# Four stages of a two-layer perceiver kernel rearranged: values folded into the output projection, a joined projection stage, a narrower reciprocal, another order of waits

## The chip, the core and the metric

The kernel runs on one core of one Trainium2 chip. The metric is the device time of one launch in microseconds. Before the change it is 2432.17 us, the median of three runs (2431.6 to 2434.42). TensorE is the matmul engine (PE in the profile, its weight loads PEld), VectorE is DVE, ScalarE is ACT, GpSimd is POOL, SyncE is SP.

## What is computed

128 batches of 32 tokens of width 128, all in float32, held as 32 tiles of 128 rows (4 batches each). Two layers follow one another; their parts are a gated unit over context rows, a linear attention, a block with attention over the batch and eight experts, a cross attention over 257 context rows, a clamped attention with normed queries and keys, and routed experts. The parts that the change touches:

```python
# linear attention, 16 heads of 64, x normed
q = softmax(q, axis=-2) * SCALE ; k = softmax(k, axis=-1)      # q over features, k over tokens
context = einsum('bhdn,bhen->bhde', k, v)
out = einsum('bhde,bhdn->bhen', context, q) @ w_out + b_out

# end of the batch attention block
proj = ao @ proj_weight.T ; h1 = hidden_states + proj
ln2 = layer_norm(h1, ln2_weight, ln2_bias) ; logits = ln2 @ router_weight

# cross attention: softmax of scores over 257 keys, times v, then w_out
# clamped attention: q, k of unit length, 50 * tanh(s / 50), causal softmax, times v, w_out
```

## The kernel before

All stages are written out as one instruction stream for each engine, with semaphores between engines; an engine executes its stream strictly in the written order. A stage is a block; between two blocks all engines meet. `steps(eng, n, body)` runs the first three tiles unrolled, then a hardware loop of two tiles a turn, then the last tile. `wait(eng, sem, value)` is a semaphore wait.

**stage_linear_attention** (137.7 to 541.5 us). Tile t, half h (8 heads each). TensorE per half: q (L495), transposes of the softmaxed q of the half before (L513), k (L500), o of the tile before (L546), v (L506), x transpose of the next tile in the first half (L489), y of the tile before in the second half (L553), A of the half before (L528). A is the 32 x 32 product of softmaxed k and q for each batch and head; o is v times A, 64 small products a half; y multiplies o, transposed, by w_out: eight 128x128 products accumulated. ScalarE: A copies (L602), q_T copy (L609), exp of q (L622), four o copies of 128 columns (L594), exp of k (L626), v copy (L629), x_T copy (L588). VectorE: sums, maxima, differences and reciprocals of both softmaxes (L698 to L712, L676, L681), the norm of the next tile (L666) and the residual add with statistics (L109, L111). GpSimd: bias add (L649), k norm (L645), q softmax (L656).

**stage_projection** (from 807.2 us) runs tile by tile: ScalarE stages the attention output (L1436), TensorE multiplies (L1444), VectorE adds to the hidden rows and takes statistics (L1451, L1453), GpSimd adds them to X (L1462); at the end 32 aggregations (L104). Then `deviation_phase` (square root L129, reciprocal L138), then `stage_norm_transpose`: norm (L1150), transpose (L1130), copy with weight and bias (L1142), router product (L1125) for each tile, and one eviction of all logits (L1154).

**stage_cross_attention** (to about 1750 us) runs in units of one batch, j = 0 to 3 in a tile. TensorE in a unit: scores of four head groups, each in its own 32-row strip (L2055), transposes of p of the unit before (L2113), k of the next unit (L2064), a transpose of the reciprocals (L2073) and p times v of two units before (L2077), v (L2086), and at the end x transpose (L2093), q (L2098) or y (L2105). VectorE in a unit: masked scores with their minimum for four groups (L2335), k rotations (L2324, L2325), two p_T copies (L2342), o mixed (L2355), o kept, called xat_o (L2364), and last the reciprocal of the row sums, written 32 times wide (L2348), so that its transpose lines up with o; then in one unit each the norm, the q products or the residual add. ScalarE: p_T copies (L2224), four exponentials (L2211), v copy (L2203), the last p column spread 32 wide, called p_last (L2218).

**stage_clamped_attention** (1752 to 2131.5 us). Per half, TensorE: q (L820), kv (L825), transposes of the scaled q and k of the half before (L836), then in the first half o transposes (L873) and the x transpose of the next tile (L810), in the second half y (L881); then scores of the half before (L850) and p times v of two halves before (L865). VectorE: o_norm (L1050, L1053), scale (L1033, L1036), sums of squares (L1079, L1082), in the first half the norm of the next tile (L1025), the lower bound of the sums (L1088), the q_T copy (L1044), in the second half the residual add. GpSimd: the power -1/2 of the bounded sums (L1011), the mask on p (L995), a sum of heads (L988). The x transpose waits for the norm of its tile.

Of the kernel before, what the change touches and what calls it, by code (L numbers as in the profile page):

```python
# [17 lines left out]
ALU = mybir.AluOpType  # L18
# [6 lines left out]
P = 128  # L25
# [396 lines left out]
def stage_linear_attention(nc, k, w, wo, bo, ahead):  # L422
# [5 lines left out]
    with ExitStack() as ctx:  # L428
# [15 lines left out]
        vs = [sb(f"v{i}", [P, W]) for i in range(2)]  # L444
        am = [sb(f"A_T{i}", [P, HALF, S]) for i in range(2)]
        oT = [sb(f"o_T{i}", [P, 2, NC, P]) for i in range(2)]
# [6 lines left out]
        pQ, pK, pV, pQT = k.bank[0:4]  # L453
        pB = k.bank[4:8]
        OC, MC = slice(0, P), slice(P, 2 * P)
        pA, pX, pY = pB[0:2], pB[2], pB[3]
# [5 lines left out]
        q_made, k_made, v_made = sem("q_made"), sem("k_made"), sem("v_made")  # L462
# [4 lines left out]
        v_copied = sem("v_copied")  # L467
# [3 lines left out]
        o_made, o_copied = sem("o_made"), sem("o_copied")  # L471
# [3 lines left out]
        block = ctx.enter_context(nc.Block())  # L475

# [8 lines left out]
        def _(pe):  # L485
            def x_transpose(t, slot):
                pe.wait_ge(normed, t + 1)
                wait(pe, o_copied, BT * (2 * (t - 1) - 1))
                pe.transpose(pX[:, MC], xn[slot][:, :], k.ident[:, :]).then_inc(turned, 1)  # L489
# [14 lines left out]
            def v(t, slot, h):  # L504
                wait(pe, v_copied, unit(t, h))
                pe.matmul(pV[:, :], xT[slot][:, :], w[:, 2, h, :], start=True, stop=True).then_inc(v_made, 1)  # L506
# [9 lines left out]
            def a(t, h):  # L516
# [4 lines left out]
                wait(pe, o_copied, BT * u)  # L521
                pe.sem_inc(pe_waited, 1)
                for i in range(NC):
                    for half in range(2):
                        r = slice(DH * half, DH * half + DH)
                        for b in range(BT):
                            n = slice(S * b, S * b + S)
                            m = pe.matmul(pA[half][n, P + i * S:P + (i + 1) * S], ks[h][r, i, n], qT[h][r, i, n],  # L528
# [4 lines left out]
            def o(t, h):  # L533
                u = unit(t, h)
                pe.wait_ge(v_copied, u + 1)
                pe.wait_ge(a_copied, 2 * u + 2)
                if h == 0:
                    wait(pe, added, 2 * (t - 1) + 1)
                wait(pe, o_copied, BT * u)
                pe.sem_inc(pe_waited, 1)  # L540
                for c in range(NC):
                    for b in range(BT):
                        n = slice(S * b, S * b + S)
                        for half in range(2):
                            hd = 2 * c + half
                            m = pe.matmul(pB[b][DH * half:DH * half + DH, c * S:(c + 1) * S],  # L546
                                          vs[h][n, hd * DH:(hd + 1) * DH], am[h][n, hd, :], start=True, stop=True)
                m.then_inc(o_made, 1)

            def y(t, slot):  # L550
                pe.wait_ge(o_copied, BT * (2 * t + 2))
                for c in range(2 * NC):
                    m = pe.matmul(pY[:, MC], oT[slot][:, c // NC, c % NC, :], wo[:, c, :],  # L553
                                  start=(c == 0), stop=(c == 2 * NC - 1))
                m.then_inc(y_made, 1)

            def body(t, slot, first, last):
                if first:
                    x_transpose(t, slot)
                for h in range(2):  # L560
# [5 lines left out]
                    if not first:  # L566
                        o(t - 1, h)
                    v(t, slot, h)
                    if h == 0 and not last:
                        x_transpose(t + 1, 1 - slot)  # L570
                    if h and not first:
                        y(t - 1, 1 - slot)
                    if h or not first:
                        a(*before)
                if last:
                    q_transpose(t, 1)
                    o(t, 0)
                    a(t, 1)
                    o(t, 1)
                    y(t, slot)  # L580
# [3 lines left out]
        def _(act):  # L584
            def x_copy(t, slot):
                act.wait_ge(turned, t + 1)
                wait(act, v_made, 2 * (t - 2) + 2)
                act.activation(xT[slot][:, :], pX[:, MC], ACT.Copy).then_inc(xt_ready, 1)  # L588

            def o_copy(t, slot, h):  # L590
                act.wait_ge(o_made, unit(t, h) + 1)
# [2008 lines left out]
```

## Time and profile before

| | |
|---|---|
| median of three runs | 2432.17 us (2431.6 to 2434.42) |
| profiled execution | 2431.76 us, span 2429.8 us |
| TensorE busy | 2207.0 us, 91% |
| VectorE busy | 1645.9 us, 68% |
| ScalarE busy | 1320.6 us, 54% |
| GpSimd busy | 1025.0 us, 42% |
| granted TensorE clock, mean | 0.946 |

Busy times come from one profiled execution; the span is that of its instructions, and the time around it (1.96 us) is not in any row. Matmuls are pipelined and the ends of their rows are modelled, so a step's price on TensorE is read from the start of its first instruction to the start of the next step's. A float32 product appears as two instructions. A row of the time-ordered view has its start, its length, the engine, the line and the operation, and in brackets the idle time of the engine before it with what ended it. A granted clock of 1.00 is 2.4 GHz, 0.50 is 1.2 GHz.

### The profile page before, as it was taken

Reading aid. Unit: us, or ns where it says so; the run is one execution under the profiler, and the core shown is the slowest. Engines: PE = TensorE matmul, PEld = TensorE weight load, DVE = VectorE, ACT = ScalarE, POOL = GpSimd, SP = SyncE. Lnnn points to the kernel's source line nnn. Section 1 sums busy time; section 2 is a strip of 40 time slices with the busy share of each in tenths; the row PEclk is TensorE's granted clock in tenths of the full one; section 3 lists DMA queues with packets and bytes.
Section 4 is the critical chain, followed back from the end, with each engine's and each line's share of the span. In section 5 each row is a group of like instructions: output and inputs, shape, how many; then the busy total and the mean of one; then the engine's idle time right before and its main releaser. Section 6 shows DMA issues by size and latency. Waiting matters only on the chain. (4 is left out here: it accounts for less than half of the span.)

```text
span 2429.8 us, 85043 instructions
## 1 busy us (share of the span) xinstructions
PE 2207.0 (91%) x30116; PEld 1628.0 (67%) x30117; DVE 1645.9 (68%) x4710; ACT 1320.6 (54%) x3760; POOL 1025.0 (42%) x925
## 2 busy tenths in 40 slices
PE   7989999989999899988999999999889999886993
PEld 4657777766888677765666666666556666664991
DVE  4577777766777543347999999999767666642441
ACT  3555555556777543335777777777555555431330
POOL 1023333325777300006555555555266666522124
PEclk8999999998999599998999999999899999978996
DMA  6630000000000000001111111111130000000112
GB/s 163 174 105 1 0 0 0 0 1 1 0 0 0 1 1 0 0 4 44 35 33 33 33 33 33 33 33 33 60 133 0 0 0 0 1 15 25 43 40 69
DMA packets 41209, 71.55 MB, mean 29 GB/s; under 512 B 6176, under 2 KB 30624, under 8 KB 40480
## 3 DMA queue, kind: packets, MB, share of 16 engines
q1 hardware_dynamic: 37792, 63.55, 8.8%
q0 software_dynamic: 3328, 6.82, 0.9%
q8 instruction: 55, 0.90, 0.2%
q14 instruction: 34, 0.28, 0.0%
HBM read 60.91 MB, written 9.44 MB: 29 GB/s over the span
## 5 line engine op out<-in xcount | busy, mean ns | idle before, releaser
L2211 ACT ACTIVATE xat_scores<-xat_scores,xat_least 128x257 f32<-128x257 f32 x512 | 258.7, 505 | 68.8 <-DVE xat_least L2335 68.5
L2335 DVE CUSTOM_DVE_ANT_0 xat_scores<-bank,xat_mask_b 128x257 f32<-128x257 f32 x512 | 205.5, 420 | 47.6 <-PE bank L2055 47.4
L2113 PE MATMUL bank<-ident,xat_scores 128*128 128x128 f32 x1024 | 189.0, 287 | 1.0 <-ACT xat_p_T L2224 0.6
L1011 POOL TENSOR_TENSOR gqa_rnorm<-gqa_norm_min,gqa_minus_half 128x12 f32<-128x12 f32 x64 | 145.8, 2278 | 103.6 <-DVE gqa_norm_min L1088 103.6
L2113 PEld LDWEIGHTS bank<-ident,xat_scores 128*128 128x128 f32 x1024 | 116.3, 141 | 83.0 <-issue 59.0
L656 POOL TENSOR_TENSOR lin_q_softmax<-lin_q_exp,lin_q_rsum 128x512 f32<-128x512 f32 x64 | 66.7, 1042 | 246.9 <-DVE lin_q_rsum L712 246.9
L1629 DVE SCALAR_TENSOR_TENSOR X<-bank,expert_shares,X 128x128 f32 (+1 forms) x256 | 71.8, 344 | 131.1 <-PE bank L1543 131.1
L2224 ACT ACTIVATE xat_p_T<-bank 128x256 f32<-128x256 f32 x256 | 96.0, 375 | 112.2 <-PE bank L2113 112.0
L1566 ACT ACTIVATE moe_gelu<-bank 128x512 f32<-128x512 f32 x128 | 76.4, 597 | 146.0 <-PE bank L1533 146.0
L1359 POOL TENSOR_TENSOR bat_scores<-bat_scores,bat_max 128x512 f32<-128x512 f32 x128 | 131.7, 1039 | 56.0 <-DVE bat_max L1391 54.2
L1543 PEld LDWEIGHTS bank<-moe_w,moe_gelu 128*128 128x128 f32 x1024 | 124.2, 192 | 30.8 <-issue 18.2
L1238 PEld LDWEIGHTS bank<-bat_v_ones,bat_p_T 128*128 128x128 f32 x1024 | 127.2, 195 | 24.1 <-ACT bat_p_T L1304 23.5
L1238 PE MATMUL bank<-bat_v_ones,bat_p_T 128*128 128x9 f32 x1024 | 128.6, 253 | 0.3 <-DVE bat_o L1399 0.3
L1543 PE MATMUL bank<-moe_w,moe_gelu 128*128 128x128 f32 x1024 | 124.6, 275 | 0.3 <-DVE expert_shares L1616 0.3
L1386 DVE TENSOR_TENSOR bat_scores<-bank,bat_causal_add 128x512 f32<-128x512 f32 x128 | 87.7, 686 | 54.6 <-PE bank L1220 48.2
L1533 PE MATMUL bank<-ln_T,moe_w 128*128 (+1 forms) x256 | 122.8, 604 | 0.8 <-PEq L1108 0.8
L2348 DVE RECIPROCAL xat_p_rsum<-xat_p_sum 128x128 f32<-128x128 f32 x128 | 120.5, 942 | 0.0
L2267 POOL TENSOR_TENSOR xat_ctx_kept<-xat_keep,xat_ctx_T 128x1028 f32<-128x1028 f32 x32 | 71.0, 2220 | 84.6 <-DMA xat_ctx_T<-in_ctxT 84.6
L2342 DVE COPY xat_p_T<-bank 128x256 f32<-128x256 f32 x256 | 106.4, 416 | 0.2 <-PE bank L2113 0.2
L2291 POOL TENSOR_SCALAR xat_keep<-xat_pad 128x1028 f32<-128x1028 uint8 x1 | 1.6, 1552 | 237.6 <-DMA xat_pad<-in_xat_pad 237.6
L2055 PE MATMUL bank<-xat_k_cos,xat_q_blocks 32*128 32x257 f32 x1024 | 92.7, 431 | 7.5 <-DVE xat_least L2335 2.7
L2211 ACT ACTIVATION_READ_ACCUMULATOR xat_scores<-xat_scores,xat_least 128x1 f32 x512 | 97.3, 190 | 0.0
(308 smaller groups left out, 6109.7 us busy)
## 6 DMA issues: line engine op xcount, KB each, us to landing
glu_ctx_N<-in_ctxN SPq DMA_DIRECT2D x32, 576.0 KB, 4.4
xat_ctx_T<-in_ctxT SPq DMA_DIRECT2D x32, 516.0 KB, 3.5
xat_pad<-in_xat_pad SPq DMA_DIRECT2D x32, 128.5 KB, 3.3
expert_w<-in_glx_w SPq DMA_DIRECT2D x1, 4096.0 KB, 15.6
slot_rows<-gqa_zero_rows SPq DMA_DIRECT2D x1, 2560.0 KB, 11.8
slt_rows<-slot_rows SPq DMA_DIRECT2D x40, 64.0 KB
slot_results<-slt_y POOLq DMA_DIRECT2D x40, 64.0 KB, 1.8
moe_w<-in_moe_w SPq DMA_DIRECT2D x2, 1024.0 KB
```

The source lines that it names most:

```text
L1011: pool.tensor_tensor(rn[h][:, :], sm[h][:, :], half_neg[:, :], ALU.pow).then_inc(rnorm, 1)
L1238: m = pe.matmul(pO[:, o:o + V1], pt[g][:, i * P:(i + 1) * P], va[slot][:, g, :], start=True, stop=True)
L1359: pool.tensor_tensor(sx[g][:, :, :], sx[g][:, :, :], spread(mx[g][:, :], P), ALU.subtract).then_inc(s_shifted, 1)
L1533: pe.matmul(pH[e % 2][c][:, :], w1[:, e, c * P:(c + 1) * P], k.LT[:, ts(b, TB), :], start=True, stop=True).then_inc(h_made, 1)
L1543: m = pe.matmul(pY[e % WAYS][:, i * D:(i + 1) * D], ge[e % 2][:, c, i * P:(i + 1) * P], w2[:, e, c, :], start=(c == 0), stop=(c == NF - 1))
L2055: m = pe.matmul(pS[g][:, 0:J], qb[slot][r, part, j, :, :], keys[j % 2][r, :], start=(part == 0), stop=(part == 1))
L2113: m = pe.transpose(dst[:, c * P:(c + 1) * P], sx[j % 2][:, g, c * P:(c + 1) * P], k.ident[:, :])
L2211: act.activation(sx[j % 2][:, g, :], sx[j % 2][:, g, :], ACT.Exp, bias=mn[j % 2][g][:, 0:1], scale=-1.0, accum_out=sm[j % 2][:, g:g + 1]). ...
L2224: act.activation(pt[j % 2][g][:, :], unit_bank(*at)[:, 0:NC * P], ACT.Copy).then_inc(pa_copied, 1)
L2335: dve.tensor_tensor_reduce(sx[j % 2][:, g, :], pS[g][:, 0:J], mb[slot][:, j, :], 1.0, BIG, ALU.add, ALU.min, mn[j % 2][g][:, 0:1]).then_in ...
L2342: dve.tensor_copy(pt[j % 2][g][:, :], unit_bank(*at)[:, 0:NC * P]).then_inc(pd_copied, 1)
L2348: dve.reciprocal(rs[j % 2][:, :, :], spread(sm[j % 2][:, :], 32)).then_inc(recip, 1)
```

## The change

Four edits.

1. Linear attention. In the first tile, TensorE transposes the value weights and multiplies them with w_out into sixteen 128x128 matrices (`wv_out`), ScalarE evicts them with the scale. The v product, its copy and o are gone. GpSimd copies the normed x of each tile; z multiplies it with A (four products of 32 rows and 256 columns, one for each batch of the tile), ScalarE evicts four times 256 columns, and y multiplies z by the new matrices: eight products after each half, the second eight one tile later. The residual add moves to the second half.
2. Clamped attention. VectorE runs scale before o_norm, and the norm of the next tile after the q_T copy.
3. The projection, the deviation, the norm, the transposes and the router product are one stage in groups of four tiles. It reads the attention output without staging.
4. Cross attention. VectorE's reciprocal is 128x4; ScalarE spreads it to 128x128 (`r_copy`), first thing in its unit.

```diff
@@ stage_linear_attention, TensorE
-            def v(t, slot, h):
-                pe.matmul(pV[:, :], xT[slot][:, :], w[:, 2, h, :], start=True, stop=True).then_inc(v_made, 1)
+            def z(t, slot, h):
+                u = unit(t, h)
+                pe.wait_ge(x_kept, t + 1)
+                pe.wait_ge(a_copied, 2 * u + 2)
+                wait(pe, z_copied, BT * u)
+                pe.sem_inc(pe_waited, 1)
+                for b in range(BT):
+                    n = slice(S * b, S * b + S)
+                    m = pe.matmul(pZ[b][:, ZC], xk[slot][n, :], am[h][n, :, :], start=True, stop=True)
+                m.then_inc(z_made, 1)
+            def y(t, slot, h):
+                pe.wait_ge(z_copied, BT * (unit(t, h) + 1))
...
+                for i in range(HALF):
+                    hd = HALF * h + i
+                    m = pe.matmul(pY[:, 0:D], zT[slot][:, hd, :], wvo[:, hd // 2, hd % 2, :],
+                                  start=(hd == 0), stop=(hd == H - 1))
...
                     kk(t, slot, h)
-                    if not first:
-                        o(t - 1, h)
-                    v(t, slot, h)
+                    if first:
+                        wv_out(h)
+                    else:
+                        if h == 0:
+                            pe.wait_ge(m_copied, 4)
+                        z(t - 1, 1 - slot, h)
+                    if h and not first:
+                        y(t - 1, 1 - slot, 0)
+                    if h == 0 and third(t):
+                        y(t - 2, slot, 1)
                     if h == 0 and not last:
                         x_transpose(t + 1, 1 - slot)
-                    if h and not first:
-                        y(t - 1, 1 - slot)
...
                 if last:
                     q_transpose(t, 1)
-                    o(t, 0)
+                    y(t - 1, 1 - slot, 1)
+                    z(t, slot, 0)
                     a(t, 1)
-                    o(t, 1)
-                    y(t, slot)
+                    y(t, slot, 0)
+                    z(t, slot, 1)
+                    y(t, slot, 1)
@@ stage_linear_attention, ScalarE and GpSimd
                 for b in range(BT):
-                    act.activation(oT[slot][:, h, :, S * b:S * b + S], pB[b][:, OC].rearrange("p (c n) -> p c n", n=S),
-                                   ACT.Copy).then_inc(o_copied, 1)
+                    act.activation(zT[slot][:, HALF * h:HALF * h + HALF, S * b:S * b + S],
+                                   pZ[b][:, ZC].rearrange("p (g n) -> p g n", n=S), ACT.Copy).then_inc(z_copied, 1)
...
-                    act.activation(vs[h][:, :], pV[:, :], ACT.Copy, scale=SCALE).then_inc(v_copied, 1)
+                    if first:
+                        wvo_copy(h)
...
+                pool.tensor_copy(xk[slot][:, :], xn[slot][:, :]).then_inc(x_kept, 1)
@@ stage_clamped_attention, VectorE
                 for h in range(2):
                     u = unit(t, h)
+                    if h or not first:
+                        scale(*ago(t, h, 1))
                     if not first and not (h == 0 and isinstance(t, int) and t < 2):
                         o_norm(*ago(t, h, 3))
-                    if h or not first:
-                        scale(*ago(t, h, 1))
...
-                    if h == 0 and not last:
-                        norm(t + 1, 1 - slot)
                     dve.wait_ge(ssum, 2 * u + 2)
...
                     if h or not first:
                         qt_copy(*ago(t, h, 1))
+                    if h == 0 and not last:
+                        norm(t + 1, 1 - slot)
@@ stage_projection, new
+            y(0)
+            y(1)
+            for g in range(NG):
+                turn(g)
+                if g + 2 < NG:
+                    y(g + 2)
+                if g:
+                    logits(g - 1)
+            logits(NG - 1)
...
+            root(0)
+            for g in range(NG):
+                if g + 1 < NG:
+                    root(g + 1)
+                copy(g)
...
+            def add(g):
+                dve.wait_ge(made, g + 1)
+                dve.tensor_tensor(k.HID[:, span(g), :], k.HID[:, span(g), :],
+                                  pY[g % 2][:, :].rearrange("p (t d) -> p t d", d=D), ALU.add).then_inc(hid_added, 1)
+                dve.wait_ge(hid_added, g + 1)
+                for t in tiles(g):
+                    dve.bn_stats(k.BNS[:, t, :], k.HID[:, t, :]).then_inc(stats, 1)
+                for t in tiles(g):
+                    dve.wait_ge(stats, t + 1)
+                    dve.bn_aggr(k.MV[:, t, :], k.BNS[:, t, :]).then_inc(aggregated, 1)
+            def norm(g):
+                dve.wait_ge(rooted, g + 1)
+                dve.reciprocal(k.RSTD[:, span(g)], k.SD[:, span(g)]).then_inc(rstd_ready, 1)
+                dve.wait_ge(rstd_ready, g + 1)
+                wait(dve, turned, g - 1)
+                for i, t in enumerate(tiles(g)):
+                    dve.tensor_scalar(xr[g % 2][:, i, :], k.HID[:, t, :], k.MV[:, t, 0:1], k.RSTD[:, t:t + 1],
+                                      ALU.subtract, ALU.mult).then_inc(normed, 1)
+            add(0)
+            for g in range(NG):
+                if g + 1 < NG:
+                    add(g + 1)
+                norm(g)
@@ stage_cross_attention, ScalarE and VectorE
+            def r_copy(t, slot, j):
+                u = BT * t + j
+                act.wait_ge(recip, u + 1)
+                wait(act, no_made, u - 1)
+                act.activation(rw[j % 2][:, :, :], spread(rs[j % 2][:, :], 32), ACT.Copy).then_inc(r_spread, 1)
...
                     one, two = ago(t, slot, j, 1), ago(t, slot, j, 2)
+                    if more:
+                        r_copy(*two)
                     if some:
                         t_copy(*one, 0, (j, T0))
...
-                dve.reciprocal(rs[j % 2][:, :, :], spread(sm[j % 2][:, :], 32)).then_inc(recip, 1)
+                dve.reciprocal(rs[j % 2][:, :], sm[j % 2][:, :]).then_inc(recip, 1)
```

## Rows read from the trace of the kernel before

**Rows 1.** Busy time by stretch: us, then PE, PEld, DVE, ACT, POOL, clock, DMA.
```profile
137.70:541.50 403.80, 389.06 (x9760) 284.60 (x9760) 309.50 (x640) 230.17 (x673) 144.95 (x160) 0.99 0.03 9
807.20:857.10 49.90, 40.73 (x160) 33.40 (x161) 28.65 (x130) 25.81 (x67) 14.56 (x33) 0.50 0.00 0
1097.00:1750.00 653.00, 611.15 (x6619) 442.65 (x6619) 581.47 (x2080) 457.86 (x1600) 359.63 (x220) 0.99 0.11 33
1755.00:2131.50 376.50, 340.42 (x7199) 222.33 (x7198) 252.88 (x639) 188.71 (x512) 237.48 (x192) 0.98 0.07 26
```

**Rows 2.** TensorE's instructions in time order, one tile of linear attention: start us, us.
```profile
303.39 1.13 PE L495 MATMUL bank<-lin_w_qkv,lin_xT 128*128 128x512 f32 x2
...
305.77 0.86 PE L546 MATMUL bank<-lin_A_T,lin_v 32*64 32x32 f32 x64
...
306.56 1.13 PE L506 MATMUL bank<-lin_w_qkv,lin_xT 128*128 128x512 f32 x2
...
307.53 2.04 PE L553 MATMUL bank<-lin_w_out,lin_o_T 128*128 128x128 f32 x16
...
309.49 0.76 PE L528 MATMUL bank<-lin_q_T,lin_k_exp 64*32 64x32 f32 x64
```

**Rows 3.** TensorE in cross attention, in time order: scores in four row strips.
```profile
1307.15 0.72 PE L2055 MATMUL bank<-xat_k_cos,xat_q_blocks 32*128 32x257 f32 x8
...
1307.69 0.61 PE L2055 MATMUL bank<-xat_k_sin,xat_q_blocks 32*128 32x257 f32 x8
```

**Rows 4.** ScalarE in clamped attention: two 128x256 reads of PSUM, in time order.
```profile
1932.02 0.38 ACT L959 ACTIVATE gqa_squares<-bank 128x256 f32<-128x256 f32 x1 [0.17 <-PE bank L825]
...
1932.30 0.38 ACT L963 ACTIVATE gqa_v_ones<-bank 128x256 f32<-128x256 f32 x1
```

**Rows 5.** The stretch of rows 2 on ScalarE and VectorE; in brackets the idle time before.
```profile
307.44 0.63 ACT L626 ACTIVATE lin_k_exp<-lin_k_exp 128x512 f32<-128x512 f32 x1
...
311.34 0.69 DVE L698 TENSOR_REDUCE lin_q_max<-bank 128x8 f32<-128x512 f32 x1 [0.91 <-PE bank L495]
```

**Rows 6.** TensorE at the end of linear attention, in time order.
```profile
536.83 3.78 PE L553 MATMUL bank<-lin_w_out,lin_o_T 128*128 128x128 f32 x16 [0.88 <-ACT lin_o_T L594]
```

**Rows 7.** VectorE from the projection to the router's logits, in time order.
```profile
832.80 0.29 DVE L1453 BATCH_NORM_STATS2 bn_stats<-hidden 128x6 f32<-128x128 f32 x1
...
833.12 2.22 DVE L104 BATCH_NORM_AGGREGATE mean_var<-bn_stats 128x2 f32<-128x6 f32 x32
...
837.93 8.30 DVE L1150 TENSOR_SCALAR attn_T<-hidden,mean_var,rstd 128x128 f32<-128x128 f32 x32 [0.33 <-PEq L121]
...
856.38 0.42 DVE L1154 COPY logits<-bank 128x256 f32<-128x256 f32 x1 [10.15 <-PE bank L1125]
```

**Rows 8.** Cross attention in time order: ScalarE, VectorE, TensorE.
```profile
1302.49 0.31 ACT L2218 ACTIVATE xat_p_last<-xat_scores 128x128 f32<-128x128 f32 x1
...
1301.96 0.94 DVE L2348 RECIPROCAL xat_p_rsum<-xat_p_sum 128x128 f32<-128x128 f32 x1
...
1304.27 0.43 DVE L2335 CUSTOM_DVE_ANT_0 xat_scores<-bank,xat_mask_b 128x257 f32<-128x257 f32 x1 [0.45 <-PE bank L2055]
...
1311.72 0.32 PE L2093 MATMUL bank<-ident,xat_xn 128*128 128x128 f32 x1 [0.17 <-DVE xat_o L2364]
...
1312.04 0.71 PE L2055 MATMUL bank<-xat_k_cos,xat_q_blocks 32*128 32x257 f32 x8
```

**Rows 9.** Clamped attention in time order: TensorE, then VectorE.
```profile
1930.96 1.02 PE L825 MATMUL bank<-gqa_w_kv,gqa_xT 128*128 128x512 f32 x2
...
1932.13 0.88 PE L836 MATMUL bank<-ident,gqa_qk_unit 128*128 128x128 f32 x6
...
1939.61 0.46 PE L850 MATMUL bank<-gqa_q_T,gqa_k_T 64*32 64x64 f32 x32 [0.44 <-DVE gqa_q_T L1044]
...
1938.45 0.34 DVE L1025 TENSOR_SCALAR gqa_xn<-X,mean_var,rstd 128x128 f32 x1
...
1938.78 0.68 DVE L1044 TENSOR_TENSOR gqa_q_T<-bank,gqa_gamma_product 128x512 f32<-128x512 f32 x1
```

More of the change, by code:

```diff
@@ L502, in kk, with wv_transpose, wv_out @@
                 m.then_inc(k_made, 1)
-            def v(t, slot, h):
-                wait(pe, v_copied, unit(t, h))
-                pe.matmul(pV[:, :], xT[slot][:, :], w[:, 2, h, :], start=True, stop=True).then_inc(v_made, 1)
+            def wv_transpose():
+                for c in range(2 * NC):
+                    pe.transpose(pZ[c // NC][:, c % NC * P:(c % NC + 1) * P],
+                                 w[:, 2, c // NC, c % NC * P:(c % NC + 1) * P], k.ident[:, :]).then_inc(wv_turned, 1)
+            def wv_out(g):
+                pe.wait_ge(wv_copied, 2)
+                for c in range(NC):
+                    for half in range(2):
+                        r = slice(DH * half, DH * half + DH)
+                        pe.matmul(pM[g][half][:, c * P:(c + 1) * P], wvT[r, NC * g + c, :], wo[r, NC * g + c, :],
+                                  start=True, stop=True).then_inc(m_made, 1)
             def q_transpose(t, h):
@@ L693, in body @@
                         k_recip(u - 1, 1 - h)
-                    if h == 0 and (not isinstance(t, int) or t >= 2):
+                    if h and third(t):
                         add(t - 2)
@@ L1424, in sem @@
             return k.semaphore("prj_" + name)
-        at = [sb(f"o_T{i}", [P, P]) for i in range(2)]
-        pY = k.bank[0:2]
-        staged, made, chain, summed = (sem(n) for n in (
-            "o_staged", "made", "chain", "x_summed"))
-        block = ctx.enter_context(nc.Block())
+        xr = [sb(f"rows{i}", [P, W, D]) for i in range(2)]
+        pY, pT, pL = k.bank[0:2], k.bank[2:4], k.bank[4]
+        made, hid_added, stats, aggregated, rooted, rstd_ready = (sem(n) for n in (
+            "made", "hidden_added", "stats", "aggregated", "rooted", "rstd_ready"))
@@ new lines, in stage_projection, with tiles, span, _ @@
+        normed, turned, copied, l_made, l_copied, summed = (sem(n) for n in (
+            "normed", "transposed", "copied", "logits_made", "logits_copied", "x_summed"))
+        block = ctx.enter_context(nc.Block())
+        def tiles(g):
+            return range(W * g, W * g + W)
+        def span(g):
+            return slice(W * g, W * g + W)
+        @block.tensor
+        def _(pe):
+            def y(g):
+                wait(pe, hid_added, g - 1)
+                for i, t in enumerate(tiles(g)):
+                    m = pe.matmul(pY[g % 2][:, i * D:(i + 1) * D], k.AT[:, t, :], w[:, :], start=True, stop=True)
+                m.then_inc(made, 1)
+            def turn(g):
+                wait(pe, copied, g - 1)
+                for i in range(W):
+                    pe.wait_ge(normed, W * g + i + 1)
+                    m = pe.transpose(pT[g % 2][:, i * P:(i + 1) * P], xr[g % 2][:, i, :], k.ident[:, :])
+                m.then_inc(turned, 1)
+            def logits(g):
+                pe.wait_ge(copied, g + 1)
+                for t in tiles(g):
+                    m = pe.matmul(pL[:, 8 * t:8 * t + 8], k.LT[:, t, :], wr[:, :], start=True, stop=True)
+                m.then_inc(l_made, 1)
+            y(0)
[7 more added lines that the diff above has]
+            logits(NG - 1)
@@ L1463, in _ @@
-            steps(pool, NT, body)
+            for g in range(NG):
+                pool.wait_ge(hid_added, g + 1)
+                pool.tensor_tensor(k.X[:, span(g), :], k.X[:, span(g), :], k.HID[:, span(g), :], ALU.add)\
+                    .then_inc(summed, 1)
 def first_of(dve, link, tmp, onehot, values, top, down):
```

138 lines of the change are left out of this document (67 added, 71 removed).

## The prediction

> **What bounds the kernel now.** The page's engine shares (TensorE 91% busy, VectorE 68%) mix stages, so I read first the busy times by stretch and then, in each of the four stretches that the diff touches, the time-ordered rows for the wait that ends last. In linear attention TensorE is busy 389.06 of 403.80 us and VectorE only 309.50 [rows 1]: its own instructions set the pace. The 49.90 us from the projection to the router's logits run at half clock, no engine is full, and the work is two short loops and a norm in sequence [rows 1]. In cross attention VectorE looks full, 581.47 of 653.00 us, and so does TensorE [rows 1]; clamped attention has slack on all engines [rows 1], so there only the order of waits counts.
>
> **Linear attention: fewer matmul columns, more eviction.** The steady tile loses v and o and gains z and a second y. TensorE's price of a step is the distance to the next step's start. v (512 columns) costs 307.53 - 306.56 = 0.97 us, o costs 306.56 - 305.77 = 0.79, twice a tile each: 3.52 us go. y costs 309.49 - 307.53 = 1.96 for eight products; sixteen are now needed, so 1.96 is added [rows 2]. z is, per half tile, four products of 32 rows by 128 weight columns and 256 moving columns, one in each row strip and bank. The trace has none; the nearest row is a cross attention score, four products of 32 x 128 by 257 columns, also one for each strip and bank: 1307.69 - 1307.15 = 0.54 us for the four [rows 3]. I take 0.54. If strips did not overlap, the price would be that of 1024 full-width columns, twice 0.97 = 1.94 [rows 2]; that is the other end. Tile: -3.52 + 1.96 + 2 x 0.54 = -0.48; over some 30 steady tiles -14 us.
>
> What hides the rest? ScalarE drops two v copies and makes eight z copies of 256 columns instead of eight of 128. Two 128x256 reads of PSUM follow each other at 1932.30 - 1932.02 = 0.28 and last 0.38 [rows 4], so four take 3 x 0.28 + 0.38 = 1.22 (1.52 if nothing overlaps). They start some 3.3 us after q (k_exp, which follows the old copies, starts 307.44 - 303.39 = 4.05 after q [rows 2, 5]; the old four lasted about 0.8), so they end near 4.5. The A products and x transpose that wait for them come after q, transposes, k, z and a y: 2.38 (o's old start, 305.77 - 303.39) + 0.54 + 1.96 = 4.88 after q [rows 2, 3]. The copies stay hidden, by 0.35 us. The Trainium skill, "TensorEngine Tiling (Array Packing)", PSUM Bottleneck, warns against just this: tiling makes TensorE faster, not the reading of PSUM, so the copies may become the bottleneck. The row's 0.28 keeps them hidden; what would follow if they were not is rival (d). k_exp slips by about 0.35, and with it VectorE's k sum, on a VectorE that waits 0.91 us for q [rows 5]; the add moves to the other half, which balances the two. GpSimd's new copy of x falls on an engine busy for 144.95 of 403.80 us [rows 1]; behind it are queued the k norm and q softmax of its queue, which A and the transposes need. I give it nothing.
>
> Ends of the stage. The first tile has eight transposes, two VectorE evictions and 32 short products before or between its own work: +2 us (0 to 5). The last tile now runs y(30,1) before z and A, and two z copies of 1.22 in place of about 0.8: 1.96 + 2 x 0.4 + hops, +3.4; y(31,1) alone stays as long as the old y, which ran 3.78 us there at half clock [rows 6]. Stage: -14.4 + 5.4 = **-9 us** (-14 to 0).
>
> **Projection, deviation, norm and router in one stage.** What goes: 32 ScalarE stagings, two stage boundaries, the single passes. What comes is a chain, since TensorE issues y(g+2) only after the transposes of group g, and these need norm(g). Per group: y(g+2) at half clock, half of eight products, 3.78 / 2 = 1.9 [rows 6]; VectorE's add, 128x512 with a PSUM operand, 0.69 [rows 5]; four statistics 0.29 each, a little overlapped, 0.9; four aggregations 0.3 (32 take 2.22); reciprocal and hops 0.35; four norms 1.1 (32 take 8.30) [rows 7]; last transpose 0.4. That is 5.7, six times 34. Before the chain: two y's, add(0), add(1), norm(0), about 7.6; after it norm(7), transpose, copy, two sets of logits and the eviction of 0.42 [rows 7], about 5. Together 47 to 48 against 49.9, since the logits end at 856.80 [rows 7]: **-2 us** (-9 to +2). GpSimd's wide adds and the logits of the group before run under VectorE's part of the chain; if that were not so, each group would cost a further 1 us.
>
> **Reciprocals of cross attention.** VectorE's 128x128 reciprocal takes 0.94 [rows 8]; a 128x4 one costs about 0.2, so VectorE loses 0.74 in each of 128 units, 95 us of busy time. ScalarE gets a 128x128 copy from a broadcast, as the p_last copy, 0.31 [rows 8], at the head of its unit, ahead of the p_T copy. But the reciprocal is the last large step of VectorE's unit, and behind it VectorE idles 0.45 us until the scores are made [rows 8]; before it, TensorE waits for xat_o, which does not depend on it [rows 8]. The loop is scores, four minima, xat_o, next TensorE step: the reciprocal is not in it. Only the unit with the norm behind the reciprocal has no such idle; I give 0.07 a tile there: **-2 us** (-6 to +4, where the copy delays p_T).
>
> **Order in clamped attention.** Two moves. scale ahead of o_norm: the transposes of q and k start 1932.13 - 1930.96 = 1.17 after kv where 512 columns need 0.97 [rows 2, 9]; the half with y gains 0.2. In the half with x_transpose nothing is gained: the scores wait for q_T, and q_T stands behind the same sum of VectorE work. There the norm moves behind q_T. Today the norm starts at 1938.45, q_T at 1938.78 ends at 1939.46, and the scores start at 1939.61, ended by q_T [rows 9]. TensorE's queue is strict: x_transpose stands ahead of the scores and waits for the norm. The norm will end 0.3 to 0.4 after q_T, and from an x transpose to the scores behind it I read 1312.04 - 1311.72 = 0.32 [rows 8]. So the scores come about 0.4 to 0.5 later in that half. Net +0.28 a tile (-0.2 to +0.6), 30 tiles: **+8.5 us** (-6 to +18).
>
> **Sum.** -9 - 2 - 2 + 8.5 = -4.5. The profiled execution took 2431.76 (span 2429.8 and 1.96 around it), 0.4 under the median of the runs: 2427.3 against it, **2428** against the median. About 0.2%, 4.9 us, is what can be told from no change.
>
> **Rivals.** (a) *The norm's new place costs nothing.* For it: the scores wait for q_T today, not for x_transpose. Then only 0.2 x 30 = 6 is gained in that stage: -9 - 2 - 2 - 6, 2413. (b) *The joined stage gets the full clock.* Rows show 0.50 throughout [rows 1]; its y's would be 0.98 instead of 1.9 six times: 6 us less, 2422. Against: TensorE was busy 40.73 of 49.90 us there and stayed at 1.2 GHz [rows 1]. (c) *Slower: x_transpose holds more than itself.* ScalarE's x copy stands before tanh, and the second half of the p products waits for tanh. It decides if the x copy is not done when the scores are (margin about 0.2 us). Then the half loses 0.8 rather than 0.45, and the stage pays about 0.6 x 30 = 18 instead of 8.5: 2438. (d) *Evictions bind in linear attention*: if four z copies take 1.52 [rows 4], k_exp and the k sum come 0.7 late, VectorE's slack, which the slip of 0.35 and the shorter halves have already cut to some 0.3 by my estimate, is used up in both halves, and the tile gains 0.15 instead of 0.48: +10, 2438. This is what the rule of the Trainium skill named above would make of the stage. (e) *Strips do not overlap*: 2 x 1.4 more a tile, 2.8 x 30, 2512. The score rows speak against it [rows 3]. (f) *The reciprocal buys time*, as VectorE's busy share suggests: say 0.4 in each of 64 of the 128 units, -25, 2404; the idle behind the reciprocal speaks against it [rows 8].
>
> **Chances.** Forecast 0.40 (its own range 2422 to 2433, half of it within 0.2%), (a) 0.18, (b) 0.12, (c) 0.13, (d) 0.10, (e) 0.02, (f) 0.05. To leave out no more than 2 in 10 the range runs from (a) to (c): 2413 to 2438. Faster by over 0.2%: (a), (b), (f) and a quarter of the forecast, 0.45; within: 0.33, from the forecast and some of (d); slower: 0.22.
>
> **What would show each step.** Linear: z at about 0.54 us from its start to the next, a 16-instruction y in both halves, half tiles near 5.9 and 5.5, VectorE still waiting for q. Projection stage: y groups some 5.7 us apart, clock 0.50. Cross attention: VectorE's idle before the minima grows by about 0.7, the stage's length stays within 2 us. Clamped attention: x_transpose close behind the norm and after q_T, the tile 0.3 longer. The prediction is wrong if the clamped tile is shorter than before, or if the linear tile is not shorter by 0.4.

## The result and the profile after

The changed kernel takes 2422.64 us, median of ten runs (2419.93 to 2428.21), beside 2433.34 (2429.26 to 2435.34) for the kernel before: ratio 0.9959, 95% interval 0.995 to 0.9967, about 10 us faster. The forecast was 4 us faster.

Busy time by stretch of the changed kernel, one row for each of [rows 1] (us, then PE, PEld, DVE, ACT, POOL, clock, DMA): linear attention with the square roots behind it, the joined projection stage, cross attention, clamped attention.

```profile
138.20:528.52 390.32, 375.02 (x6600) 297.38 (x6600) 312.65 (x646) 225.45 (x616) 152.55 (x192) 0.99 0.03 9
791.50:835.70 44.20, 32.80 (x161) 30.22 (x161) 24.53 (x114) 9.98 (x18) 10.21 (x9) 0.62 0.00 1
1068.10:1726.90 658.80, 612.67 (x6624) 443.13 (x6624) 499.50 (x2091) 485.13 (x1731) 361.28 (x221) 0.98 0.12 34
1728.70:2119.60 390.90, 334.44 (x7200) 225.81 (x7200) 260.18 (x640) 193.37 (x514) 238.83 (x192) 0.98 0.07 25
```

Between the same marks of the two traces (from the first norm of a stage to the square root behind it; the projection stage from its start to the end of the logits' eviction; the routed experts from the last square root to the end of the span):

| stage | before | after | difference | forecast |
|---|---|---|---|---|
| linear attention | 406.4 | 390.3 | -16.1 | -9 |
| projection to logits | 49.6 | 43.8 | -5.8 | -2 |
| cross attention | 660.8 | 658.8 | -2.0 | -2 |
| clamped attention | 379.8 | 390.9 | +11.1 | +8.5 |
| routed experts (untouched) | 296.8 | 298.7 | +1.9 | 0 |
| span | 2429.8 | 2418.3 | -11.5 | -4.5 |

The rest, -0.6, is spread over the untouched stages. A stage whose instructions are the same moves by up to 4 us between the traces of two kernels (routed experts 296.8 to 299.8, but for the three traces of the last section; cross attention with the narrow reciprocal 657.2 to 661.2), so a stage's difference of that size is not a finding by itself. The -2.0 of cross attention is none.

**Linear attention**, TensorE in time order, the tile that answers to [rows 2] (start us, us):

```profile
302.88 1.12 PE L504 MATMUL bank<-lin_w_qkv,lin_xT 128*128 128x512 f32 x2
...
305.26 0.71 PE L559 MATMUL bank<-lin_A_T,lin_x_kept 32*128 32x256 f32 x8
305.91 2.05 PE L568 MATMUL bank<-lin_w_v_out,lin_z_T 128*128 128x128 f32 x16
307.80 0.27 PE L498 MATMUL bank<-ident,lin_xn 128*128 128x128 f32 x1
308.00 0.76 PE L546 MATMUL bank<-lin_q_T,lin_k_exp 64*32 64x32 f32 x64
...
311.07 0.71 PE L559 MATMUL bank<-lin_A_T,lin_x_kept 32*128 32x256 f32 x8
311.72 2.05 PE L568 MATMUL bank<-lin_w_v_out,lin_z_T 128*128 128x128 f32 x16
313.70 0.76 PE L546 MATMUL bank<-lin_q_T,lin_k_exp 64*32 64x32 f32 x64
```

z costs 305.91 - 305.26 = 0.65, y 1.89 ahead of the x transpose and 1.98 ahead of A, and no row waits: TensorE still sets the pace. ScalarE and VectorE in the same tile: the four z copies take 1.21, and VectorE still waits for q.

```profile
311.85 1.21 ACT L620 ACTIVATE lin_z_T<-bank 128x256 f32<-128x256 f32 x4
...
309.85 0.69 DVE L737 TENSOR_REDUCE lin_q_max<-bank 128x8 f32<-128x512 f32 x1 [0.37 <-PE bank L504]
```

TensorE at the end of the stage, where [rows 6] had a last y of 3.78:

```profile
518.81 2.05 PE L568 MATMUL bank<-lin_w_v_out,lin_z_T 128*128 128x128 f32 x16
520.79 0.71 PE L559 MATMUL bank<-lin_A_T,lin_x_kept 32*128 32x256 f32 x8
522.84 2.05 PE L568 MATMUL bank<-lin_w_v_out,lin_z_T 128*128 128x128 f32 x16 [1.33 <-ACT lin_z_T L620]
```

**Projection stage**, one group in time order: VectorE's add, statistics, reciprocal and norm, TensorE's transposes of group g, then the products of g+2.

```profile
805.52 0.69 DVE L1533 TENSOR_TENSOR hidden<-hidden,bank 128x512 f32<-128x512 f32 x1 [1.71 <-PE bank L1486]
806.25 0.87 DVE L1537 BATCH_NORM_STATS2 bn_stats<-hidden 128x6 f32<-128x128 f32 x4
807.03 0.36 DVE L1540 BATCH_NORM_AGGREGATE mean_var<-bn_stats 128x2 f32<-128x6 f32 x4
807.31 0.14 DVE L1544 RECIPROCAL rstd<-std 128x4 f32<-128x4 f32 x1
807.49 1.12 DVE L1548 TENSOR_SCALAR prj_rows<-hidden,mean_var,rstd 128x128 f32<-128x128 f32 x4
807.99 1.15 PE L1493 MATMUL bank<-ident,prj_rows 128*128 128x128 f32 x4 [0.99 <-DVE prj_rows L1548]
808.94 1.92 PE L1486 MATMUL bank<-prj_w,attn_T 128*128 128x128 f32 x8
810.89 0.69 DVE L1533 TENSOR_TENSOR hidden<-hidden,bank 128x512 f32<-128x512 f32 x1 [2.28 <-PE bank L1486]
...
814.20 1.38 PE L1486 MATMUL bank<-prj_w,attn_T 128*128 128x128 f32 x8
815.62 0.69 DVE L1533 TENSOR_TENSOR hidden<-hidden,bank 128x512 f32<-128x512 f32 x1 [1.64 <-PE bank L1486]
```

Here is the serial chain: each engine waits for the other, from add to add 5.37 and 4.73 us. And the clock is not 0.50 throughout (windows of the same stage; the clock is the third number from the end):

```profile
805.00:811.00 6.00, 5.00 (x26) 4.78 (x24) 3.13 (x15) 1.09 (x3) 1.26 (x1) 0.50 0.00 0
811.00:815.00 4.00, 2.59 (x18) 2.24 (x18) 2.91 (x14) 0.90 (x2) 1.26 (x1) 0.93 0.00 0
815.00:821.00 6.00, 5.01 (x25) 4.79 (x25) 3.03 (x15) 1.25 (x3) 1.26 (x1) 0.50 0.01 3
```

It rose to 2.4 GHz behind a stretch in which TensorE was busy for 5.00 of 6.00 us, and was back at 1.2 behind one with 2.59 of 4.00: one such turn for two groups.

**Clamped attention**, TensorE and VectorE in time order, the half that answers to [rows 9]:

```profile
1907.17 1.12 PE L859 MATMUL bank<-gqa_w_q,gqa_xT 128*128 128x512 f32 x2 [0.22 <-issue]
...
1911.29 0.33 PE L849 MATMUL bank<-ident,gqa_xn 128*128 128x128 f32 x1 [0.95 <-DVE gqa_xn L1064]
1911.59 0.46 PE L889 MATMUL bank<-gqa_q_T,gqa_k_T 64*32 64x64 f32 x32
...
1913.17 1.13 PE L859 MATMUL bank<-gqa_w_q,gqa_xT 128*128 128x512 f32 x2
...
1917.11 0.46 PE L889 MATMUL bank<-gqa_q_T,gqa_k_T 64*32 64x64 f32 x32 [0.41 <-DVE gqa_q_T L1083]
...
1910.29 0.69 DVE L1083 TENSOR_TENSOR gqa_q_T<-bank,gqa_gamma_product 128x512 f32<-128x512 f32 x1
1910.89 0.34 DVE L1064 TENSOR_SCALAR gqa_xn<-X,mean_var,rstd 128x128 f32 x1
```

The x transpose now waits 0.95 us for the norm, which stands behind the q_T copy, and the scores stand behind the x transpose. All waits of the x transpose for the norm in the stage, in the view of waits (engine, line, releaser: us in total, times, longest), the changed kernel first, then the kernel before:

```profile
PE bank L849 <- DVE gqa_xn L1064: 32.4, 32, 5.9
```

```profile
PE bank L810 <- DVE gqa_xn L1025: 7.5, 3, 5.9
```

**Cross attention**: the groups of VectorE's minima (xcount, then busy and mean ns, then idle before), of the kernel before and of the changed one.

```profile
L2335 DVE CUSTOM_DVE_ANT_0 xat_scores<-bank,xat_mask_b 128x257 f32<-128x257 f32 x512 | 205.5, 420 | 47.6 <-PE bank L2055 47.4
```

```profile
L2447 DVE CUSTOM_DVE_ANT_0 xat_scores<-bank,xat_mask_b 128x257 f32<-128x257 f32 x512 | 205.6, 421 | 98.4 <-PE bank L2157 98.4
```

VectorE's busy time fell by 86 us between the stage's marks, from 585.46 to 499.50; more than half of that, 50.8 us, came back as idle time in front of the minima, and the stage is 2 us shorter.

### The profile page after: what moved, and what is told of

Same layout as the page of the kernel before. It is cut to its first block and busy times, and to the rows that moved or that the text cites. A ratio compares the mean times of both kernels' runs of the same rounds, so it can differ in the third digit from the quotient of the medians.

```text
span 2418.3 us, 78420 instructions
## 1 busy us (share of the span) xinstructions
PE 2174.5 (90%) x26956; PEld 1637.5 (68%) x26957; DVE 1565.4 (65%) x4695; ACT 1326.3 (55%) x3779; POOL 1029.1 (43%) x933
## 5 line engine op out<-in xcount | busy, mean ns | idle before, releaser
L568 PEld LDWEIGHTS bank<-lin_w_v_out,lin_z_T 128*128 128x128 f32 x1024 | 119.1, 191 | 22.0 <-issue 20.2
L568 PE MATMUL bank<-lin_w_v_out,lin_z_T 128*128 128x128 f32 x1024 | 131.2, 281 | 1.3 <-ACT lin_z_T L620 1.3
L1072 DVE TENSOR_TENSOR gqa_qk_unit<-bank,gqa_rnorm 128x512 f32<-128x512 f32 x64 | 44.3, 691 | 89.5 <-POOL gqa_rnorm L1050 89.5
```

The source lines that it names most:

```text
L568: m = pe.matmul(pY[:, 0:D], zT[slot][:, hd, :], wvo[:, hd // 2, hd % 2, :], start=(hd == 0), stop=(hd == H - 1))
```

## The experiments

The theory: the stages are independent, each moved by what its own slowest loop gained or lost. Its rivals are the prediction's cases.

**One edit undone at a time.** Three kernels have the changed kernel with one part as it was.

> The changed kernel with linear attention as it was. Theory (the fold is the gain): the stage goes from 390.3 back to 406.4 us, this kernel is 16 us slower than the changed one, ratio to the kernel before 1.002 to 1.003. Rival (part of those 16 us is chance of the two profiled executions, as the forecast of 9 would have it): 9 us slower, ratio 0.999 to 1.000.

Measured: ratio 1.0035 (1.0023 to 1.0046), 18 us over the changed kernel, a little more than expected; the stage took 406.8. The first edit is the gain, not chance. Without it the other edits together are a loss of 8 us. (The run undoes the edit as a whole; what the move of the residual add is worth by itself was not tried.)

> The changed kernel with the projection, the deviation and the norm with transposes and router as the three stages they were. Theory (the joined stage gains what its marks show, 49.4 to 43.8 us): 5.5 us slower than the changed kernel, ratio 0.998. Rival (as forecast, 2 us, the rest given back at the start of the experts stage): ratio 0.9965 to 0.997.

Measured: ratio 0.9976 (0.9967 to 0.9984), 4.1 us over the changed kernel's ratio, between the two expectations; from the second square root of the batch block to the logits 312.1 us, as before the change (312.2), against 306.4.

> The changed kernel with cross attention as it was (128x128 reciprocal on VectorE, no spreading copy on ScalarE). Theory (the reciprocal lies in VectorE's idle time, only the unit with the norm pays): 2 us slower than the changed kernel, ratio 0.997, VectorE's idle before the minima back from 98 us to 48 us. Rival (VectorE's busy time is what sets the stage, 0.4 us in half the units): 25 us slower, ratio 1.006.

Measured: ratio 0.9973 (0.9962 to 0.9984), 3.4 us over the changed kernel, with intervals that overlap; the stage took 659.1 against 658.8. Idle in front of the minima was back at 47.2 us. The medians give some 100 us of VectorE's reciprocals a worth of 3.4 us, the stage's marks 0.3; the case for 25 us (f) is out.

**Clamped attention: which of the two moves costs.** All moves are in VectorE's half:

```diff
@@ gqa_old
+o_norm
 scale
-o_norm
 sums of squares
+if h == 0: norm(t + 1)
 lower bound
 qt_copy
-if h == 0: norm(t + 1)
@@ gqa_norm_mid
 scale
 o_norm
 sums of squares
+if h == 0: norm(t + 1)
 lower bound
 qt_copy
-if h == 0: norm(t + 1)
@@ gqa_norm_head
+if h == 0: norm(t + 1)
 scale
 o_norm
 sums of squares
 lower bound
 qt_copy
-if h == 0: norm(t + 1)
```

> The changed kernel with clamped attention as it was (VectorE: o_norm, scale, sums of squares, norm of the next tile, lower bound, q_T copy). Theory: the reordering alone cost that stage 11.1 us (379.8 before, 390.9 after, from stage start to end in the two traces), so this kernel is 11 us faster than the changed one, ratio to the kernel before 0.991, stage 380 us. Rival (the stage is longer for a reason outside its own order, for example the state in which the earlier stages leave clock or transfers): ratio stays 0.996, stage 391.

> The changed kernel with only the norm put back ahead of the lower bound and the q_T copy; scale stays ahead of o_norm. Theory (the norm's place is the whole cost): the scores of the first half start 0.83 after the q_T copy starts instead of 1911.59 - 1910.29 = 1.30, the q_T copy 0.1 later: 0.38 less a tile, 30 tiles, 11 us; ratio 0.991, as with the whole old order. Rival (o_norm behind scale is what costs, since GpSimd's sum of heads then comes later): ratio 0.995 to 0.996. Rival of the prediction (scale first gains 0.2 in the half with y, on top): stage 374, ratio 0.989.

> The changed kernel with the norm of the next tile at the head of VectorE's half, ahead of scale, where VectorE idles 1.2 to 1.6 us for GpSimd's power. Theory: the norm is then free and the q_T copy does not stand behind it; scores of the first half 0.47 earlier than in the changed kernel, 14 us, ratio 0.990. Rival (the loop is closed by GpSimd's power, 2.28 us, not by VectorE's order): no faster than with the norm ahead of the lower bound, 0.991 or more.

Measured, in this order: 0.9909 (0.9894 to 0.9924), 0.9928 (0.9914 to 0.9941) and 0.9911 (0.9898 to 0.9925); stages of 378.3, 379.7 and 380.2 us against 390.9. The norm's place is the whole cost: by the stage's marks each place ahead of the q_T copy gives 11 to 13 us back. (By the ratios it is 12, 8 and 12 us: the second kernel's ratio misses the expected 0.991, its stage does not.) Scale ahead of o_norm gains nothing: 379.7 is no shorter than 378.3. TensorE in gqa_norm_mid, the kernel with that move alone, shows why; the half with y:

```profile
1908.37 1.12 PE L859 MATMUL bank<-gqa_w_q,gqa_xT 128*128 128x512 f32 x2
...
1912.44 0.46 PE L889 MATMUL bank<-gqa_q_T,gqa_k_T 64*32 64x64 f32 x32 [0.54 <-DVE gqa_q_T L1083]
```

The kernel before, the same half and the q of the next:

```profile
1930.00 1.12 PE L820 MATMUL bank<-gqa_w_q,gqa_xT 128*128 128x512 f32 x2
...
1934.04 0.46 PE L850 MATMUL bank<-gqa_q_T,gqa_k_T 64*32 64x64 f32 x32
...
1935.62 1.12 PE L820 MATMUL bank<-gqa_w_q,gqa_xT 128*128 128x512 f32 x2
```

The scores come 4.07 us after q, against 1934.04 - 1930.00 = 4.04 before the change. The transposes do start earlier, but the scores wait for q_T, behind scale, o_norm and sums in whatever order. The third kernel came out as its rival had it, 0.991 and no faster than with the norm ahead of the lower bound: a norm in VectorE's idle time did not bring q_T forward (its start is 3.13 us after q's, 3.12 in the changed kernel).

**Linear attention: do the z copies bind?** More reads of a z bank, ahead of the last z copy, into a spare tile; one a half in the first run, three in the second. Nothing else uses the spare tile.

```diff
@@ z_copy
+                    if b == 2:
+                        for i in range(n):
+                            act.activation(spare[:, h, i, :], pZ[3][:, ZC], ACT.Copy).then_inc(spared, 1)
```

> The changed kernel with one more ScalarE read of a z bank (128x256) into a spare tile in each half of linear attention, ahead of the last z copy: 0.28 us more of eviction before the exponential of k, 64 times. Theory (the copies are hidden: VectorE still waits 0.37 to 0.65 us for q in each half): the stage stays within 3 us of 390.3, ratio 0.996 to 0.997. Rival (evictions already bind, the prediction's case d): 0.28 x 62 = 17 us more, ratio 1.003.

> The changed kernel with three more reads of a z bank in each half of linear attention, 0.84 us. One more cost 3.6 us in the stage. Theory (a slack of some 0.25 us in the half with the residual add, of 0.6 in the other, that the change leaves over): (0.84 - 0.25) x 31 + (0.84 - 0.6) x 31 = 26 us more in the stage than the changed kernel, 416 us, ratio 1.006. Rival (no slack, each read costs itself): 0.84 x 62 = 52 us, ratio 1.017.

Measured: with one, ratio 0.9981 (0.9973 to 0.999), the stage 393.9, 3.6 us more, just over the 3 expected and far from the rival's 17; with three, 1.0123 (1.0108 to 1.0139), the stage 423.8, 33.5 us more, where 26 were expected and 52 by the rival. If the first 0.28 us cost 3.6/62 = 0.06 a half, and the next 0.56 cost (33.5 - 3.6)/62 = 0.48, the slack is by this estimate some 0.25 to 0.3 us a half, then nearly all is paid. With one read more, VectorE goes from the add straight into the maximum of q with no idle time, where the changed kernel had 0.37:

```profile
310.10 0.29 DVE L111 BATCH_NORM_STATS2 bn_stats<-X  x1
310.53 0.69 DVE L742 TENSOR_REDUCE lin_q_max<-bank 128x8 f32<-128x512 f32 x1
```

Over the stage, VectorE's mean idle time in front of the maximum of q, in the half of a tile where it is shorter, is 0.64 us in the kernel before, 0.3 in the changed one (there it is the half with the residual add) and 0.07 with one read more. So the copies do not bind, but by 0.3 us only. The Trainium skill, "TensorEngine Tiling (Array Packing)", PSUM Bottleneck, warns that the copies out of PSUM may become the bottleneck when tiling has made TensorE faster; the runs bear it out as a warning. The copies did not become it, and with three reads more the trace has TensorE waiting for them (0.26 us ahead of an x transpose, 0.27 ahead of A).

**Projection: break the chain.** TensorE issues the products of g+2 ahead of the transposes of g:

```diff
-        pY, pT, pL = k.bank[0:2], k.bank[2:4], k.bank[4]
+        pY, pT, pL = k.bank[5:8], k.bank[2:4], k.bank[4]
...
             for g in range(NG):
-                turn(g)
                 if g + 2 < NG:
                     y(g + 2)
+                turn(g)
```

> The changed kernel with a third bank for the projection's products, and TensorE issuing the products of group g+2 before the transposes of group g, not behind them. Theory (the stage is one serial chain of 5.26 or 4.8 us a group: products 1.95, add 0.72, statistics 0.79, aggregation 0.28, reciprocal 0.18, first norm 0.50, transposes 0.84): the products leave the chain, a group then costs what TensorE has to do at half clock, 1.9 + 1.15 + 1.3 = 4.35, or what VectorE has to do, 3.1, at full clock: the stage is 5 to 12 us shorter, ratio 0.991 to 0.994. Rival (TensorE, busier, is held at half clock through the whole stage, and the router products of the group before now delay the products): within 2 us of the changed kernel, ratio 0.995 to 0.997.

Measured: ratio 0.9895 (0.9882 to 0.9909), 15 us under the changed kernel, more than the range expected; the stage to the logits 13.9 us shorter (292.5 against 306.4). TensorE in time order, and the clock:

```profile
806.63 1.14 PE L1486 MATMUL bank<-prj_w,attn_T 128*128 128x128 f32 x8
807.97 1.01 PE L1493 MATMUL bank<-ident,prj_rows 128*128 128x128 f32 x4 [0.20 <-DVE prj_rows L1548]
808.82 0.96 PE L1499 MATMUL bank<-moe_router,ln_T 128*128 128x8 f32 x8
```

```profile
808.00:810.00 2.00, 2.00 (x15) 1.70 (x16) 1.97 (x8) 0.78 (x1) 0.73 (x1) 1.00 0.00 0
```

A group now takes 3.00 us, VectorE's own work (1.97 of 2.00 us busy), and the granted clock stays at 1.00, 2.4 GHz, from 804 to 818 us. Two things came together: TensorE's waits shrank to 0.20 us, and at the full clock its part fits under VectorE's. No run separates them.

**The repairs together.** both is the changed kernel with clamped attention's old order and the products ahead (three banks); both_two_banks keeps two banks; both_xat_old also has the wide reciprocal.

> The changed kernel with clamped attention's old order and with the projection's products ahead of the transposes: the two repairs together. Theory (the stages are independent, gains add): 11.4 + 15.2 = 26.6 us under the changed kernel's 2422.6, 2396 us, ratio 0.985. Rival (part of either gain was chance or is given back in the next stage): ratio 0.988 or more.

> The kernel with both repairs, but with two banks for the projection's products as in the changed kernel: only the order on TensorE differs, products of group g+2 ahead of the transposes of group g. Theory (the order made the chain, the bank did not: the products of g+2 wait for the add of group g, which VectorE has done before the norm of g-1): as with three banks, stage to the logits 292.7 us after the second square root of the batch block, ratio 0.985. Rival (with two banks the wait for the add stands in front of the transposes and remakes the chain in part): 3 to 8 us longer, ratio 0.9865 to 0.9885.

> The kernel with both repairs, and cross attention as it was (wide reciprocal on VectorE). Second measurement of that edit, against the run beside it. Theory (only the unit with the norm pays): 0 to 3.5 us slower than the run beside it, ratio 0.985 to 0.9865; the same stage of 658 to 660 us in both traces. Rival (the reciprocal is worth some 25 us): ratio 0.995.

Measured: 0.9853 (0.9838 to 0.9868), 0.9854 (0.9837 to 0.987) and 0.9852 (0.9838 to 0.9866). The gains add, and the order alone made the chain: two banks do as well (to the logits 293.0 against 292.7). Beside a kernel before of 2431.16, both_two_banks took 2395.33, 36 us under it; the three ratios are the best here and can't be told apart. In the second measurement the narrow reciprocal is worth nothing: the ratios differ by 0.0001, and the stage, expected at 658 to 660 us in both traces, took 661.2 with it and 659.5 without. The two measurements together leave it between 0 and some 3 us.

## Why the prediction was half right

The direction, the stages' signs and the range were right; the time was 5 us too high (2428 against 2422.64), and the gain of 10.7 us had been put at 4. That 2422.64 is also the price of case (b), 2422, is chance: most of the difference arose elsewhere. By its terms:

**Linear attention, steady tiles: -14.4 forecast, -16.8 measured.** From one A to another, both behind a y: 529.71 - 162.25 = 367.46 before, 512.61 - 161.98 = 350.63 after.

```profile
162.25 0.76 PE L528 MATMUL bank<-lin_q_T,lin_k_exp 64*32 64x32 f32 x64
...
529.71 0.76 PE L528 MATMUL bank<-lin_q_T,lin_k_exp 64*32 64x32 f32 x64
```

```profile
161.98 0.76 PE L546 MATMUL bank<-lin_q_T,lin_k_exp 64*32 64x32 f32 x64
...
512.61 0.76 PE L546 MATMUL bank<-lin_q_T,lin_k_exp 64*32 64x32 f32 x64
```

Term by term z was too cheap (0.65, not 0.54: +0.2 a tile), and two gains were missing: the second y costs 1.89, not 1.96, and from the x transpose to A it is 0.20 us where it was 0.38 to 0.43 behind v. Away from the loop's turns the tile went from 12.0 to 11.5 us; over the 30 tiles it is 16.83/30 = 0.56, the rest lying at the turns. The mechanism was right. Case (e), strips that do not overlap, is refuted by z at 0.65; case (d), binding evictions, by the runs above, with 0.3 us to spare, which is what the prediction had left of VectorE's slack in that case.

**The stage's ends: +5.4 forecast, +1.2 measured.** This is the step that failed in linear attention. From its first instruction to A at 162, TensorE needs 162.25 - 138.25 = 24.00 before and 161.98 - 138.17 = 23.81 after. The added transposes and products did cost what was forecast: the A in front of that one starts at 156.29, 1.8 us later than before.

```profile
154.50 0.75 PE L528 MATMUL bank<-lin_q_T,lin_k_exp 64*32 64x32 f32 x64
```

```profile
156.29 0.75 PE L546 MATMUL bank<-lin_q_T,lin_k_exp 64*32 64x32 f32 x64
```

But the next half tile, which the forecast had not counted among the steady ones, is 2.06 us shorter (5.69 against 7.75): z is there in place of o and v, 1.1, and a pause of 0.81 in q that the trace before has there is gone. At the stage's end it was +1.4 instead of +3.4 (10.90 from A to the last y's end before, 12.28 after), mostly because the last y takes 2.05 where it took 3.78 [rows 6]. The forecast took 3.78 over, a price at half clock. In the kernel before the granted clock was 0.50 from 535 to 541 us, after a stretch (530 to 535) in which TensorE was busy for 2.87 of 5.00 us. In the changed one, with y(30,1) and y(31,0) there too, it was busy for 3.47 and 3.56 of 5.00 us in the last two stretches (515 to 525), and the clock stayed at 1.00, although the idle time right in front of the last y is longer, 1.33 against 0.88 us. Steady tiles and ends together are -15.6 of the stage's -16.1; the other 0.5 lies outside these marks.

**Projection: -2 forecast, -5.8 measured.** The chain was found rightly. Its period was put at 5.7; it is 5.10 on average (five periods, products starting at 798.78 to 824.28). Of these 0.6, some 0.3 are the clock: in every other group the products run in part at 2.4 GHz, and from their start to the add it is 1.28 to 1.48 us (814.20 to 815.62 in the rows above) where the others take 1.95. The rest is small terms: statistics 0.79 and not 0.9; reciprocal and hops 0.18 and not 0.35, since the square root of a group has long been there; norm and transposes 1.34 to 1.45 and not 1.5. The add's 0.69 was right, though [rows 5] has it from a maximum of the same size. Six groups at 0.6 less are 3.6 of the missing 3.8; and the prediction's own terms add up to 7.6 + 34.2 + 5 = 46.8 us, which would have been -2.8. So case (b) came true in part, with 1.7 of its 6 us, against the argument that a stretch busy for 40.73 of 49.90 us had stayed at 1.2 GHz. What the forecast did not ask is why the chain should be there at all; breaking it was worth more than twice the joined stage's own gain. The Trainium skill, "TensorE: Matmul & The Clock Gate", HAM oscillation — how this bites in real kernels, describes a loop whose wait for a transfer puts the clock back in every turn. The trace of the changed stage agrees that a loop's waits go with a clock that falls again and again (0.50, 0.93, 0.50), but here it rose and fell once in two groups, with waits for VectorE of 1.0 to 1.4 us; with waits of 0.20 us it stayed at 1.00.

**Cross attention: -2 forecast, 0 to 3 measured.** Right: the reciprocal was not in the loop. Case (f) is refuted by two runs.

**Clamped attention: +8.5 forecast, +11.1 measured.** The loss was right to its size: in the half with the x transpose the scores come 1911.59 - 1907.17 = 4.42 after q, where 1939.61 [rows 9] - 1935.62 = 3.99 was the old distance: +0.43, forecast 0.4 to 0.5. The 0.2 that scale ahead of o_norm should gain in the other half is the step that failed: 1917.11 - 1913.17 = 3.94 against 4.04 here (3.94 against 4.00 as means over the stage), and nothing in the kernel that has that move alone. The forecast read a late start of the transposes as late scores, without asking what else the scores wait for. Case (c) did not come: tanh starts 0.57 us after the scores do, as before the change, so the x copy does not hold it, and the stage paid 11, not 18. Case (a) is refuted.

**Sum.** -16.1 - 5.8 - 2.0 + 11.1 = -12.8 in the four stages, -11.5 in the span, -10.7 in the medians. The forecast's two largest errors are the ends (4.2 us) and the projection (3.8). Some 3.4 of these 8 us are costs taken at a half clock that was no longer there, the last y and the products of every other group. The larger loss in clamped attention (2.6) hid part of the errors.

## What to carry to other kernels

A step that is put behind another on one engine is priced by whoever waits for it in order elsewhere: the norm cost nothing on VectorE and 11 us on TensorE, whose scores stood behind its transpose. When a stage is fused into groups, write the chain down and ask which instruction stands in it only because of its place in a queue; issuing the next group's products one step earlier was worth 14 us where the fusion gave 6. And an engine's busy time is no forecast: 86 us less on VectorE gave between 0 and some 3, while on ScalarE the fold had 0.3 us a half to spare, and 0.84 us more a half turned its gain into a loss.

## What the runs showed of the hardware

The clock of a short stage can change with the order of its instructions alone. The same 160 instructions of TensorE ran at a mean granted clock of 0.62 in the changed kernel, with waits of 1.0 to 1.4 us ahead of the transposes in most groups, and at 0.84 with the products ahead, three banks or two; in 14 of these 30 us it was 1.00, with waits of 0.20.

One stage changed from session to session, whatever the kernel. The kernel before took 2393.08 us beside both, both_xat_old and the kernel with three more reads, and 2431 to 2434 beside the others. The chip's number on record does not explain it: it is 7 for those three runs and also for gqa_old, beside which the kernel before took 2432.41. Nearly all of it lies in the routed experts, 258.7 to 259.3 us in those three traces and 296.8 to 299.8 in all others. TensorE there, in a stretch of 40 us that begins some 40 us after the last square root, the changed kernel first, then both:

```profile
2160.60:2200.60 40.00, 16.26 (x63) 9.61 (x61) 3.35 (x5) 2.39 (x4) 26.93 (x29) 0.74 0.16 55
```

```profile
2136.90:2176.90 40.00, 40.00 (x188) 25.54 (x187) 13.29 (x20) 8.96 (x15) 28.20 (x30) 1.00 0.15 52
```

TensorE was idle for 24 us in the one and for none in the other, while the transfers moved 55 and 52 GB/s. In the changed kernel's trace its longest waits in this stage, 18.1, 15.3 and 12.8 us, are for one tile of VectorE (glx_gh); in that of both the longest wait for it is 1.8. What holds it there was not tried; each ratio compares kernels of one session, so the ratios do not see it.
